# Two self attentions of a fused six-layer kernel: values mixed ahead of the scores, and the rotation made of unnormed numbers out of the bank

## What is computed

```python
q, k, v = split(x_normed @ w_qkv)            # 16 heads of 32
q = q * rsqrt(mean(q*q) + EPS) * q_gamma     # per head
k = k * rsqrt(mean(k*k) + EPS) * k_gamma
q = q * cos + rotate_half(q) * sin           # rotation by position
k = k * cos + rotate_half(k) * sin
scores = where(causal, q @ k.T / sqrt(32), NEG)
x = x + (softmax(scores) @ v) @ w_out
```

## Time and profile before

| | us |
|---|---|
| median of 3 runs | 2281.76 (2281.2 to 2282.37) |
| the profiled execution | 2280.83 |
| its span in the profile | 2279.0 |
| L0a in the trace | about 461 to 624 |
| L1a in the trace | about 1515 to 1715 |

### The profile page before, as it was taken

The page is one execution under the profiler, slowest core; times in us unless marked ns, Lnnn a source line. Parts: engine busy times, 40 slices in busy tenths (PEclk is TensorE's granted clock), DMA queues, the critical chain, the costliest instruction groups (busy, mean ns, idle before and its releaser), DMA issues.

```text
span 2279.0 us, 28145 instructions
## 1 busy us (share of the span) xinstructions
PE 2097.8 (92%) x8874; PEld 1406.9 (62%) x8874; DVE 1162.8 (51%) x2688; ACT 785.7 (34%) x1978; POOL 977.2 (43%) x937
## 2 busy tenths in 40 slices
PE   7998999998888999999997999988884999999995
PEld 5865766576567864566664666657653555555553
DVE  4227777645634112355554777758755343444443
ACT  2124434323331210133334433324432444445441
POOL 1027465301156210177667465447401444455552
PEclk8998999999999999999999999999985999999998
DMA  3231001010021000011112010110034799988886
GB/s 115 82 111 54 18 25 35 31 62 1 8 104 56 32 32 1 13 38 51 40 70 88 18 28 21 66 63 1 1 120 144 243 306 297 266 214 213 218 213 167
DMA packets 84545, 209.21 MB, mean 92 GB/s; under 512 B 13857, under 2 KB 39969, under 8 KB 76929
## 3 DMA queue, kind: packets, MB, share of 16 engines
q1 hardware_dynamic: 61680, 153.54, 19.7%
q0 software_dynamic: 21280, 51.38, 10.9%
q10 hardware_dynamic: 1440, 2.49, 0.3%
HBM read 257.95 MB, written 34.36 MB: 128 GB/s over the span
## 4 chain that ended last, share of the span: by engine, by line
PE 62%; DVE 18%; ACT 9%; POOL 6%; issue 4%; DMA 2%; SPq 0%; ACTq 0%; POOLq 0%; DVEq 0%
PE banks L98 38%; PE banks L854 4%; PE banks L2277 3%; PE banks L2278 3%; PE banks L448 3%; DVE L0x_prob L541 2%; ACT L0x_prob L489 2%; ACT L1x_prob L489 2%; DVE L1x_prob L541 2%; POOL L1a_tiny L1585 2%; PE banks L2252 2%; POOL L1a_part_s L1609 2%; DVE L0x_small L528 2%; DVE L0x_pT_lo L509 2%; DVE L1x_pT_lo L509 1%
## 5 line engine op out<-in xcount | busy, mean ns | idle before, releaser
L98 PE MATMUL banks<-L1f_w,L1f_xT 128*128 x760 | 265.2, 492 | 2.4 <-ACT L1f_xT L2345 1.5
L2526 POOL DMA_INDIRECT moe_sums<-L1f_y,L1f_row x95 | 150.6, 1585 | 220.7 <-DVE L1f_is_who L2398 162.8
L159 POOL TENSOR_TENSOR rstd<-rstd,power 128x1 f32<-128x1 f32 x48 | 29.5, 615 | 420.5 <-DVE rstd L153 420.5
L98 PEld LDWEIGHTS banks<-L1f_w,L1f_xT 128*128 128x128 f32 x760 | 138.1, 192 | 82.6 <-issue 7.5
L2534 POOL DMA_INDIRECT L1f_xg<-moe_rows,L1f_row x95 | 94.1, 991 | 76.0 <-DVE L1f_row L2393 49.2
L448 PE MATMUL banks<-L0x_wn,L0x_qT 128*128 128x512 f32 x256 | 115.1, 593 | 0.8 <-DVE x L518 0.8
L448 PE MATMUL banks<-L1x_wn,L1x_qT 128*128 128x512 f32 x256 | 115.1, 593 | 0.8 <-DVE x L518 0.8
L2365 DVE SCALAR_TENSOR_TENSOR L1f_z<-banks,L1f_share,L1f_sg 128x192 f32<-128x192 f32 x95 | 39.7, 418 | 148.3 <-ACT L1f_sg L2300 148.3
L489 ACT ACTIVATE L0x_prob<-banks,L0x_small 128x256 f32<-128x256 f32 x128 | 58.9, 472 | 159.6 <-DVE L0x_small L531 159.6
L489 ACT ACTIVATE L1x_prob<-banks,L1x_small 128x256 f32<-128x256 f32 x128 | 58.9, 472 | 158.8 <-DVE L1x_small L531 158.8
L98 PE MATMUL banks<-L0f_down,L0f_z 128*128 128x512 f32 x256 | 111.1, 593 | 1.5 <-DVE L0f_z L1857 1.5
(11 more groups left out here) (393 smaller groups left out, 5304.8 us busy)
## 6 DMA issues: line engine op xcount, KB each, us to landing
L1f_w<-in_experts SPq DMA_DIRECT2D x95, 1280.0 KB
L1f_laid<-moe_counts SPq DMA_DIRECT2D x59, 512.0 KB, 5.4
w<-in_L1x_heads SPq DMA_DIRECT2D x16, 704.0 KB, 4.0
w<-in_L0x_heads SPq DMA_DIRECT2D x16, 608.0 KB, 3.8
w<-in_wug SPq DMA_DIRECT2D x8, 1024.0 KB, 4.7
L0x_craw<-in_ctx SPq DMA_DIRECT2D x96, 64.0 KB, 2.0
L1x_craw<-in_ctx SPq DMA_DIRECT2D x96, 64.0 KB, 2.0
w<-in_L0x_out SPq DMA_DIRECT2D x4, 1280.0 KB, 5.5
```

Source lines behind the costliest of these rows:

```text
L98: ins = pe.e.matmul(out, w, m, start=first and n == 0, stop=last and n == len(pairs) - 1)
L2526: pool.e.indirect_dma_start(self.sums[j % 2][:, :], bass.IndirectOffsetOnAxis(ap=self.row[:, j:j + 1], axis=0), self.y[j % self.NY][:], No ...
```

## The change

In both attentions TensorE mixes the values of tile i-5 ahead of the scores of tile i-3 and turns them ahead of queries and keys; mix_use, which sets the banks' order, follows. VectorE weighs mixed values ahead of the mask. ScalarE copies the turned values first, then queries and keys, then takes the Exp. The calls after the loop are reordered alike.

In L1a the rotation is made of unnormed numbers and the norm's root is multiplied in at the end. VectorE makes the cosine products right behind the reductions, out of banks 0 and 1 (after ScalarE's copy of the same bank), and project(i+1) waits for them instead of for the copies. GpSimd makes the sine products of the unnormed copies first in its step, then the power. VectorE adds both and multiplies by the root after spread_dve and ahead of normalise(i+2). Instruction counts stay as they were.

```diff
--- before.py
+++ after.py
@@ -1056,7 +1056,7 @@
             self.v_set = take("v_set", NT)
             self.norm_sum, self.norm_root = take("norm_sum", 3 * NT), take("norm_root", NT)
             self.turned_dve, self.turned_pool = take("turned_dve", 4 * NT), take("turned_pool", 4 * NT)
-            self.qk_set = take("qk_set", 2 * NT)
+            self.cos_set = take("qk_set", 2 * NT)
         else:
             self.qkv_set = take("qkv_set", 3 * NT)
         self.q_turned, self.k_turned = take("q_turned", NT), take("k_turned", NT)
@@ -1075,7 +1075,7 @@
         self.x_done = self.x_added if normed else self.x_biased
         self.ends = [(self.x_done, NT)]
 
-        self.projected_all = [(self.qkv_made, 3 * NT), (self.copied, 2 * NT), (self.v_set, NT), (self.qk_set, 2 * NT)] if normed else [
+        self.projected_all = [(self.qkv_made, 3 * NT), (self.copied, 2 * NT), (self.v_set, NT), (self.turned_dve, 4 * NT)] if normed else [
             (self.qkv_made, 3 * NT), (self.qkv_set, 3 * NT)]
 
         self.turned_all = [(self.pT_set, NT)]
@@ -1106,10 +1106,10 @@
 
         self.mix_use = {}
         for i in range(NT + 5):
+            if 0 <= i - 5 < NT:
+                self.mix_use["values", i - 5] = len(self.mix_use)
             if 0 <= i - 3 < NT:
                 self.mix_use["scores", i - 3] = len(self.mix_use)
-            if 0 <= i - 5 < NT:
-                self.mix_use["values", i - 5] = len(self.mix_use)
         self.mix_order = list(self.mix_use)
 
     def bank7_free(self, pe, what, i):
@@ -1156,7 +1156,7 @@
         elif which == 2:
             eng.wait_ge(self.v_set, i + 1)
         else:
-            eng.wait_ge(self.qk_set, 2 * i + which + 1)
+            eng.wait_ge(self.turned_dve, 4 * i + 2 * which + 2)
 
 
 
@@ -1223,14 +1223,14 @@
                 self.turn_input(pe, i + 1)
             if i == 1:
                 self.begin(pe)
+            if 0 <= i - 5 < NT:
+                self.mix(pe, i - 5)
             if 0 <= i - 3 < NT:
                 self.score(pe, i - 3)
             if 0 <= i - 5 < NT:
-                self.mix(pe, i - 5)
+                self.turn_values(pe, i - 5)
             if 0 <= i - 2 < NT:
                 self.spread(pe, i - 2)
-            if 0 <= i - 5 < NT:
-                self.turn_values(pe, i - 5)
             if 0 <= i - 4 < NT:
                 self.turn_weights(pe, i - 4)
             self.after.turn_early(pe, i)
@@ -1240,19 +1240,19 @@
             self.after.transform_early(pe, i)
 
         last = NT + 2
+        self.mix(pe, NT - 3)
         self.score(pe, NT - 1)
-        self.mix(pe, NT - 3)
+        self.turn_values(pe, NT - 3)
         self.turn_weights(pe, NT - 2)
         self.after.turn_early(pe, last)
         self.mix(pe, NT - 2)
-        self.turn_values(pe, NT - 3)
-        self.turn_weights(pe, NT - 1)
         self.after.ask_early(pe, last)
         self.project_out(pe, NT - 3)
         self.after.transform_early(pe, last)
+        self.turn_values(pe, NT - 2)
+        self.turn_weights(pe, NT - 1)
         self.after.turn_early(pe, last + 1)
         self.mix(pe, NT - 1)
-        self.turn_values(pe, NT - 2)
         self.after.ask_early(pe, last + 1)
         self.project_out(pe, NT - 2)
         self.after.transform_early(pe, last + 1)
@@ -1281,7 +1281,7 @@
                 elif which == 2:
                     pe.wait_ge(self.v_set, i)
                 else:
-                    pe.wait_ge(self.copied, 2 * (i - 1) + which + 1)
+                    pe.wait_ge(self.cos_set, 2 * (i - 1) + which + 1)
             accumulate(pe, self.sh.psum(which)[:, 0:n], [p for k in range(KD) for p in parts(
                 cut(self.hT[i % 3], slice(None), k, slice(None)),
                 cut(w_, slice(None), k, slice(None)))]).then_inc(self.qkv_made.sem, 1)
@@ -1351,21 +1351,16 @@
                 self.square(act, i)
             if 0 < i < NT - 1:
                 self.input_hi(act, i + 1)
+            if 0 <= i - 5 < NT:
+                self.keep_values(act, i - 5)
+            if 0 <= i - 2 < NT:
+                self.spread_keys(act, i - 2)
             if 0 <= i - 3 < NT:
                 act.wait_ge(self.shifted, i - 2)
                 pr = self.pr[(i - 3) % 2]
                 act.e.activation(pr[:], pr[:], ACT.Exp, scale=float(DH) ** -0.5).then_inc(self.exped.sem, 1)
-            if 0 <= i - 2 < NT:
-                self.spread_keys(act, i - 2)
-            if 0 <= i - 5 < NT - 3:
-                self.keep_values(act, i - 5)
-            if 0 <= i - 4 < NT - 1:
+            if 0 <= i - 4 < NT:
                 self.keep_weights(act, i - 4)
-            if i >= NT + 2:
-
-                self.keep_values(act, i - 5)
-            if i == NT + 2:
-                self.keep_weights(act, NT - 1)
             if 0 <= i - 2 < NT:
                 self.spread_values(act, i - 2)
             self.after.keep_early(act, i)
@@ -1440,16 +1435,19 @@
             if i < NT:
                 if self.normed:
                     self.norm_sums(dve, i)
+                    self.turn_cosines(dve, i)
                 else:
                     self.add_biases(dve, i)
             if 0 < i < NT - 1:
                 self.input_lo(dve, i + 1)
+            if 0 <= i - 5 < NT:
+                self.keep_mixed(dve, i - 5)
             if 0 <= i - 3 < NT:
                 self.mask_scores(dve, i - 3)
-            if 0 <= i - 5 < NT:
-                self.keep_mixed(dve, i - 5)
             if 0 <= i - 2 < NT:
                 self.spread_dve(dve, i - 2)
+            if i < NT and self.normed:
+                self.turn_and_norm(dve, i)
             if i + 2 < NT:
                 self.normalise(dve, i + 2)
             self.after.rows_early(dve, i)
@@ -1457,13 +1455,11 @@
                 self.sum_weights(dve, i - 3)
             if 0 <= i - 5 < NT:
                 self.add_output(dve, i - 5)
-            if i < NT and self.normed:
-                self.norm_and_turn(dve, i)
         last = NT + 2
+        self.keep_mixed(dve, NT - 3)
         self.mask_scores(dve, NT - 1)
+        self.after.rows_early(dve, last)
         self.sum_weights(dve, NT - 1)
-        self.keep_mixed(dve, NT - 3)
-        self.after.rows_early(dve, last)
         self.keep_mixed(dve, NT - 2)
         self.add_output(dve, NT - 3)
         self.after.rows_early(dve, last + 1)
@@ -1516,25 +1512,26 @@
     def across(self, ap):
         return ap.rearrange("p (o d) -> p o d", o=1).to_broadcast([P, AH, ap.shape[-1]])
 
-    def norm_and_turn(self, dve, i):
+    def turn_cosines(self, dve, i):
         for w in range(2):
-            q = self.heads(self.qkv[w][i % 3][:])
-            root = self.tiny[:, i, 2 + w, :].rearrange("p (h o) -> p h o", o=1).to_broadcast([P, AH, DH])
-            dve.wait_ge(self.norm_root, i + 1)
+
             dve.wait_ge(self.copied, 2 * i + w + 1)
-            dve.e.tensor_tensor(q, q, root, ALU.mult).then_inc(self.turned_dve.sem, 1)
-        for w in range(2):
-            dve.wait_ge(self.turned_dve, 4 * i + w + 1)
             dve.wait_ge(self.tabs_set, 2)
             if i:
-                dve.wait_ge(self.qk_set, 2 * (i - 1) + w + 1)
-            dve.e.tensor_tensor(self.part_c[w][:], self.heads(self.qkv[w][i % 3][:]), self.across(self.cosg[:, w, :]),
-                                ALU.mult).then_inc(self.turned_dve.sem, 1)
+                dve.wait_ge(self.turned_dve, 4 * (i - 1) + 2 * w + 2)
+            dve.e.tensor_tensor(self.part_c[w][:], self.heads(self.sh.psum(w)), self.across(self.cosg[:, w, :]),
+                                ALU.mult).then_inc(self.cos_set.sem, 1)
+
+    def turn_and_norm(self, dve, i):
         for w in range(2):
-            dve.wait_ge(self.turned_dve, 4 * i + 2 + w + 1)
+            root = self.tiny[:, i, 2 + w, :].rearrange("p (h o) -> p h o", o=1).to_broadcast([P, AH, DH])
+            dve.wait_ge(self.cos_set, 2 * i + w + 1)
             dve.wait_ge(self.turned_pool, 4 * i + 2 * w + 2)
-            dve.e.tensor_tensor(self.heads(self.qkv[w][i % 3][:]), self.part_c[w][:], self.part_s[w][:],
-                                ALU.add).then_inc(self.qk_set.sem, 1)
+            dve.e.tensor_tensor(self.part_c[w][:], self.part_c[w][:], self.part_s[w][:], ALU.add).then_inc(self.turned_dve.sem, 1)
+            dve.wait_ge(self.norm_root, i + 1)
+            dve.wait_ge(self.turned_dve, 4 * i + 2 * w + 1)
+            dve.wait_ge((self.q_turned, self.k_turned)[w], i - 2)
+            dve.e.tensor_tensor(self.heads(self.qkv[w][i % 3][:]), self.part_c[w][:], root, ALU.mult).then_inc(self.turned_dve.sem, 1)
 
     def spread_dve(self, dve, i):
         dve.wait_ge(self.k_turned, i + 1)
@@ -1580,6 +1577,16 @@
         pool.e.memset(self.vbd[2][:], 0.0).then_inc(self.cleared.sem, 1)
         for i in range(NT + 5):
             if i < NT and self.normed:
+                hd = DH // 2
+                for w in range(2):
+                    q = self.heads(self.qkv[w][i % 3][:])
+                    pool.wait_ge(self.copied, 2 * i + w + 1)
```

(18 more changed lines are left out.)

## The result

The changed kernel takes 2244.8 us (median; 2242.8 to 2247.46) beside 2282.07 for the kernel before on the same chip: ratio 0.9837, 95% interval 0.982 to 0.9854. Forecast was 2244.6. The profiled execution took 2247.46, its span is 2245.7, so the two profiled spans differ by 33.3 us only, where the medians differ by 37.3. Two later comparisons of the same kernels gave 34.9 us (2281.13 and 2246.25) and 36.1 (2282.7 and 2246.65).

What follows compares the result with a forecast made beforehand. TensorE, busy in 92% of the span, was taken as the bound, so only its waits and low clock could give: 14.7 + 22.4 = 37.1 us, 2280.8 - 37.1 + 0.9 = 2244.6 us, range 2238 to 2252 (chance 0.60).

Steps and rivals of the forecast that it cites:

- L0a: First self attention: reordering removes waits of 6 and 2.5 us and 6.2 us of low clock, 14.7 us in all.
- L1a to project(2): Start of the second self attention: VectorE waits for the power in tiles 0 to 2, project(2) stays at 1537.30; 0 us.
- L1a to project(4): Second self attention, i = 2 and 3: project(4) starts at 1562.0, not 1563.40; 1.4 us.
- L1a to the first output, i = 5: Second self attention: turn_weights(0) stops waiting for Exp (5.8), low clock goes (2.6), some given back; 8.4 us in all.
- i = 6, 7: Second self attention: waits of 1.72 us before the outputs become 0.6; 2.3 us.
- i = 8: Second self attention: norm_and_turn(7) no longer precedes keep_mixed; 5.0 us of waits and 0.9 for half-clock turns, 5.9.
- i = 9, to the last pair of mix and scores: Second self attention: output projection no longer at low clock, 3.0 us, and 0.3 of wait; 3.3 us.
- tail: Second self attention, behind the last score pair to the last row of x: 2.5 us, between 0 and 5.
- M: Start of TensorE's pair scores and mix; ScalarE was to copy values 4.95 us and queries 5.8 us after it.
- The rival that it stays low where it was: TensorE's clock stays low because holes of 0.6 to 0.75 us remain: gain 23 us, 2259; chance 0.16.
- my root at 1530.4: Second self attention, tile 0: GpSimd's power, after the sines, gives the norm's root at about 1530.4 us.
- My margin of 2 us in steady steps: Second self attention: GpSimd's power ends 2 us before VectorE asks in steady steps; negative in three.

Runs made afterwards that it cites:

- the order alone: Only the step order changed in both attentions, old rotation kept, against the kernel before: 2254.04 us, ratio 0.9875.
- the third execution: The changed kernel measured and traced again without edits, in a later comparison against the kernel before: 2246.65 us.
- the second execution: The changed kernel measured and traced once more without edits, beside its separated parts, against the kernel before: 2246.25 us.

## Why the prediction was right, and where it was only nearly right

By its own steps; "at" is the time since project(0), which takes out what happens ahead of the stage.

| step | forecast | measured |
|---|---|---|
| L0a | 14.7 | 15.7 |
| L1a to project(2) | 0 | 0 (at 21.74 before, now 21.77) |
| L1a to project(4) | 1.4 | 2.0 |
| L1a to the first output, i = 5 (the 1.4 is part of it) | 8.4 | 9.4 (85.93, 76.49) |
| i = 6, 7 | 2.3 | 2.5 |
| i = 8 | 5.9 | 5.7 |
| i = 9, to the last pair of mix and scores | 3.3 | 2.6 |
| tail | 2.5 | 3.2 |
| L1a in all | 22.4 | 23.6 |
| the rest of the program | 0 | -6.0 in this pair |

- **The order.** ScalarE's values and queries were forecast at M + 4.95 and M + 5.8 and came at 4.96 and 5.85. The hole in front of turn_weights is 0.74 in L1a (forecast 0.6) and 0.94 in L0a (0.75).
- **L0a.** The waits of the earlier trace rows and pTb's 0.5 came to 15.5 us; with the same three they are 8.8 now. So 6.7 went where I had 8.5, and part of the difference is the end, where mix(6) waits 1.96 for pTb and I had taken 0. The other 9 us are clock and what it slows, where I had 6.2 (TensorE's busy time fell by 8.8): every output projection now takes 3.60 to 3.70, where the earlier trace rows has 6.73.
- **The clock.** The rival that it stays low where it was fell. Holes of 0.74 and 0.94 in each step left the granted clock at 1.00 in every window of 20 us of L0a and L1a but the first of each (0.91). What it gave back was undersized: I had 14 us of clock in the 37.1, and TensorE's busy time in the two stages fell by 18.9.
- **The start of L1a.** Errors that cancelled. I had the sines at 4.6 us per tile; alone they take 1.43 + 1.44 = 2.9, and 1.90 + 2.05 = 3.95 beside VectorE. The earlier trace rows has their median at 1150 ns only because it was read beside contending products, and its least, 815, was the better guess. But the first sines start 6.0 us behind project(0) where my root at 1530.4 needs them at 4.8: the copy ended at 4.5, and a memset of GpSimd (1.81 us), which I hadn't named, stands in front. So the root comes at 14.2 where I had 14.8. The rest came back as contention: root and sum of tile 0 take 1.23 and 1.22, and normalise(2) behind them 0.95. xn is late by 0.95, a wait that I hadn't named either, and 2.83 stays of the 4.40. The Trainium skill, page "SBUF — State Buffer", section "Who interferes with whom", says that a VectorE product with one SBUF input doesn't contend: the trace agrees (cosines of 0.68 throughout, with the sines of 1511.76 at 1.44 beside them). The same section calls the shared ports an exclusive lock, and says of VectorE's two-port modes that the other engine is blocked for the whole instruction. For two SBUF inputs the rows show both sides slowed, and by less than that: 1.23 for 0.69 on VectorE while GpSimd's pair takes 1.90 for 1.43. In the earlier trace rows a VectorE product is 1.23 and a half of the sines 1.15, where taking turns would make each 0.69 + 0.73 = 1.42 (an estimate from the rows of both alone).
- **i = 8.** "keep_mixed(3) behind add_output(2), some 1.6 stay": 1.17 + 0.74 = 1.9.
- **The power.** Forecast was that VectorE waits in tiles 0 to 2; it waits in 0 and 1 (4.29, 3.16), and in tile 2 the power ends 0.6 us before VectorE asks. From tile 2 on GpSimd itself waits for ScalarE's copies (2.40). My margin of 2 us in steady steps was too small: in tiles 3 to 7 the power ends 3.3, 2.5, 3.5, 5.1 and 5.2 us ahead.
- **The signs.** I had called it wrong if project(i+1) waits for the cosines. It does once, project(1) for 0.15 us, where I had said nothing, at worst 1 us. The other signs came as forecast: cosines of 0.68, no wait of VectorE for the power past tile 3, output projections of L0a at 3.6 to 3.7. Of the powers one gap is 12.00, not 10 to 11, and the holes of L0a are 0.94, not 0.8.
- **The sum.** The two stages gave 39.3, 2.2 more than forecast, and the profiled execution lost 6.0 outside them. The forecast took 0 there. In other executions of the same kernel the stretch between is 894.6 and 897.1 against 898.3. Over the 11 traces with the new order it has a mean of 896.5, and the two with the old order have 895.2 and 895.4, so an effect of the change of about 1 us can't be excluded, and 3 us are not its doing. That the median came within 0.3 us of the forecast is luck: the stages gave 2.2 more than forecast, the rest of the program lost what I had put at nothing (6.0, 1.0 and 5.6 in the three executions), and the two later comparisons gave 34.9 and 36.1.

## What to carry to other kernels

Where an engine's queue mixes work that frees a bank with work that waits for another engine, put the freeing first: here the order of the steps, with not one instruction less, was worth 27 of the 35 us that the whole change gave on the same chip. Count the clock in: half of what TensorE gained here was not waiting but shorter matmuls. Move the start of an operation before making it cheaper: cosines that cost 0.2 us less each bought nothing that could be measured. Look behind a wait in the middle of a queue: if what the other engine needs next stands there, the two form a ring. Here a longer ring was paid in full where it was longer than TensorE's step, and cost nothing in the two steps of 19 us.

## What the runs showed of the hardware

- GpSimd's power of 128 x 32 numbers takes 5.43 us, a multiply of the same 0.25.
- The same code runs at different clocks in different executions. L0a of the changed kernel took 142.3 us where no part of it was at the low clock, and 146.7 in the kernel with the order alone, at a mean of 0.97.
- The stretch of unchanged code between the attentions takes 894.6 to 898.3 us. A part of the difference is TensorE's clock early in L0f. The first and the third execution of the same kernel have these windows of 680 to 700 us (busy time of the five engines as on the page, clock, DMA), and the product of the two high halves in L0f takes a mean of 401 and 396 ns; before it was 393.

```profile
680.00:700.00 20.00, 17.33 (x64) 13.78 (x63) 8.79 (x11) 2.14 (x3) 13.38 (x11) 0.83 0.12 38
```

```profile
680.00:700.00 20.00, 17.34 (x77) 14.06 (x76) 10.32 (x11) 2.14 (x3) 15.25 (x12) 1.00 0.05 7
```

The Trainium skill, page "TensorE: Matmul & The Clock Gate", section "What's actually happening", says that the number of matmuls at the low clock at a kernel's start varies between runs of one kernel; the traces show the same of a stretch in the middle. The clock of L0f alone doesn't explain it: the second execution has 396 ns too, and the shortest stretch. No experiment was made on what brings the dips about.
